# A routed transformer block: expert blocks of 256 rows instead of 128, and gate and placement moved behind the second turn of the attention output

## The reference

```
h = embed(x)                                  # [64, 197, 192]: 196 patches and a class token
h = h + attention(layernorm(h))               # 12 heads of 16, q and k normalised a head
x2 = layernorm(h).reshape(12608, 192)
scores = sigmoid(x2 @ gate_weight.T)          # 8 experts in 4 groups
# 2 groups by the sum of their biased scores, then the 2 best experts in them
w, idx = chosen scores over their sum, their experts
h1, h3 = x2 @ w1[e].T, x2 @ w3[e].T           # 128 wide
y = sum over the 2 chosen e of  w * (silu(h1) * h3) @ w2[e].T
z = silu(x2 @ sw1.T) * (x2 @ sw3.T) @ sw2.T   # the shared expert, every row
h = h + y + z
```

## Time and profile before

| | us |
|---|---|
| median of 3 runs (lowest, highest) | 2247.59 (2235.23, 2253.08) |
| the profiled execution, its span | 2258.84, 2257.0 |
| PE busy | 1861.1 (82%) |
| DVE, ACT, POOL busy | 1147.4, 992.2, 644.1 |
| phase A, to the first operation of the table | 1574.65 |
| the table | 18.07 |
| phase B's blocks | 664.28 |

### The profile page before, as it was taken

One profiled execution on the slowest core, in us unless ns is written; L12 is line 12 of the kernel. 1 busy time (PEld: TensorE's weight loads), 2 busy tenths in 40 slices (PEclk: granted clock), 3 DMA queues, 4 the chain that ended last, 5 costly groups with the idle time before them and its releaser, 6 DMA issues. The chain is left out here.

```text
span 2257.0 us, 56485 instructions
## 1 busy us (share of the span) xinstructions
PE 1861.1 (82%) x16989; PEld 1447.9 (64%) x16990; DVE 1147.4 (51%) x4105; ACT 992.2 (44%) x2620; POOL 644.1 (29%) x681
## 2 busy tenths in 40 slices
PE   3988889898988988989898898973677888788886
PEld 2767777776776766777677677753455555555554
DVE  3465666665765665666566566654422222222222
ACT  2544445554554544455455454540233333333333
POOL 2011121211212121121122112122244444444444
PEclk9998999999999999999899999995555555555555
DMA  4011111111111111111111111101343444443443
GB/s 140 23 39 39 53 45 44 54 53 40 51 47 46 53 43 42 53 45 53 41 46 56 42 53 45 32 27 34 58 63 61 63 62 61 62 63 59 60 63 43
DMA packets 97206, 116.35 MB, mean 52 GB/s; under 512 B 16496, under 2 KB 83700, under 8 KB 96884
## 3 DMA queue, kind: packets, MB, share of 16 engines
q1 hardware_dynamic: 55108, 74.15, 11.7%
q0 software_dynamic: 41872, 39.30, 11.0%
HBM read 63.65 MB, written 50.51 MB: 51 GB/s over the span
## 5 line engine op out<-in xcount | busy, mean ns | idle before, releaser
L1457 POOL DMA_INDIRECT out<-yb,xb x205 | 319.5, 1558 | 363.8 <-ACT yb L1357 187.8
L772 ACT ACTIVATE prob<-ps_sc 99x792 f32<-99x792 f32 x384 | 317.2, 826 | 220.0 <-PE ps_sc L532 217.1
L474 PE MATMUL ps_hid<-lin_f,xin 128*99 128x192 f32 x1536 | 305.1, 345 | 79.6 <-DVE v L927 44.8
L474 PEld LDWEIGHTS ps_hid<-lin_f,xin 128*99 128x99 f32 x1536 | 249.9, 175 | 92.6 <-issue 56.3
L1434 DVE TENSOR_TENSOR in_lo<-inner,in_hi 128x128 f16<-128x128 f32 x205 | 59.9, 292 | 478.4 <-ACT in_hi L1350 477.1
L1300 PE MATMUL ps_h<-bT_hi,w_hi 96*128 96x128 f16 x820 | 251.3, 306 | 57.1 <-issue 47.9
L1153 POOL DMA_INDIRECT dispatch<-rows,slot x256 | 254.0, 992 | 123.1 <-issue 63.1
L1301 PE MATMUL ps_h<-bT_lo,w_hi 96*128 96x128 f16 x820 | 257.2, 314 | 0.0
L1302 PE MATMUL ps_h<-bT_hi,w_lo 96*128 96x128 f16 x820 | 257.2, 314 | 0.0
L1147 POOL CAST slot<-slot_f 99x4 int32<-99x4 f32 x64 | 11.6, 181 | 821.4 <-DVE slot_f L1049 821.4
L532 PE MATMUL ps_sc<-qT,kT 32*99 32x198 f32 x3072 | 192.6, 368 | 14.5 <-issue 11.8
(11 more groups left out here) (172 smaller groups left out, 4113.6 us busy)
## 6 DMA issues: line engine op xcount, KB each, us to landing
xin<-xp SPq DMA_DIRECT2D x64, 594.0 KB, 3.9
xb<-dispatch SPq DMA_DIRECT2D x205, 98.0 KB
out<-base SPq DMA_DIRECT2D x64, 147.0 KB
dispatch<-rows,slot POOLq DMA_INDIRECT x256
out<-yb,xb POOLq DMA_INDIRECT x205
w_f<-w SPq DMA_DIRECT2D x1, 1728.0 KB, 12.1
out<-base SPq DMA_DIRECT2D x64, 0.8 KB
w_f<-w SPq DMA_DIRECT2D x1, 864.0 KB, 13.8
```

The lines of the kernel that those rows point to most:

```text
L474: last = pe.matmul(hid[:, t, :], xin[q][:, k, t * TR:(t + 1) * TR], lin_f[:, k, :], start=(k == 0), stop=(k == PCHUNKS - 1))
L772: act.activation(prob[quad][:, places].rearrange("p h m s -> p h (m s)"), ps_sc[0:TR, places, 0:2 * SLOTS], ACT.Exp, scale=D ** -0.5 / (SQ ...
L1457: pool.indirect_dma_start(tokens_out, bass.IndirectOffsetOnAxis(ap=xb[n.mod(XB)][:, ID_AT:ID_AT + 1].bitcast(I32), axis=0), yb[n.mod(4)][: ...
```

## The change

It has two independent parts.

**Blocks.** PARTS = 2 and BLOCK = 256. `xb`, `pad` and `yb` hold two rows a partition, PE turns a block with 4 transposes, its 12 inner products have 256 columns, its outer products are 6 matmuls, ACT weighs in two operations and POOL issues two indirect transfers a block; BLOCKS becomes 106, TABLE 109. XB becomes 4. The expert's number is read into a register once a block and kept (`expert_at`), ahead of the body's matmuls. Waits on `added` count 32 a block instead of 16.

**Phase A's order.** On PE, `shared_inner(n6)` comes before `qk(n2, 1)`; the third quad of scores comes a step earlier, behind `transpose_qk(n2, 0, 0)`; then `o_by_token(n4, 1)`, `places(n7)`, `gate(n6)` and `embed(k, 0)`. On ACT, `shared_sigmoid` comes before `square(n2, 1)` and `gate_exp` last. On DVE, all of `route` is for n7, its third part and `place_out` stand behind `v_copy`, and `shared_gate` and `residual` come before `qk_normalise(n2, 1)`.

```diff
-BLOCK = 128
+PARTS = 2
+BLOCK = 128 * PARTS
...
-XB = 8
+XB = 4
...
             def load(n):
                 if n.c >= XB or not n.known:
-                    sp.wait_ge(added[n.mod(2)], parity(n.back(XB), 32))
+                    sp.wait_ge(added[n.mod(2)], parity(n.back(XB), 16 + ADDS))
                 at = sp.value_load(entry(1, n), min_val=0, max_val=E * CAP)
-                sp.dma_start(xb[n.mod(XB)][:], dispatch[bass.DynSlice(at, BLOCK), :]).then_inc(x_in[n.mod(XB)], 16)
+                rows = dispatch[bass.DynSlice(at, BLOCK), :].rearrange("(p r) w -> p r w", r=PARTS)
+                sp.dma_start(xb[n.mod(XB)][:], rows).then_inc(x_in[n.mod(XB)], 16)
...
             def body(n):
+                inner_e = expert_at(n.back(1)) if n.back(1).active() else None
+                outer_e = expert_at(n.back(3)) if n.back(3).active() else None
                 if n.active():
                     turn(n)
                 if n.back(1).active():
-                    inner_products(n.back(1))
+                    inner_products(n.back(1), inner_e)
                 if n.back(3).active():
-                    outer_products(n.back(3))
+                    outer_products(n.back(3), outer_e)
...
-                act.activation(yb[q][:], outer[n.mod(2)], ACT.Copy,
-                               scale=xb[n.mod(XB)][:, W_AT:W_AT + 1]).then_inc(yb_done, 1)
+                for r in range(PARTS):
+                    last = act.activation(yb[q][:, r, :], outer[n.mod(2)][:, r, :], ACT.Copy,
+                                          scale=xb[n.mod(XB)][:, r, W_AT:W_AT + 1])
+                last.then_inc(yb_done, 1)
...
-                pool.indirect_dma_start(
-                    tokens_out, bass.IndirectOffsetOnAxis(ap=xb[n.mod(XB)][:, ID_AT:ID_AT + 1].bitcast(I32), axis=0),
-                    yb[n.mod(4)][:], None, bounds_check=TOTAL - 1, oob_is_err=False,
-                    compute_op=ALU.add).then_inc(added[n.mod(2)], 16)
+                for r in range(PARTS):
+                    ids = xb[n.mod(XB)][:, r, ID_AT:ID_AT + 1].bitcast(I32)
+                    pool.indirect_dma_start(
+                        tokens_out, bass.IndirectOffsetOnAxis(ap=ids, axis=0), yb[n.mod(4)][:, r, :], None,
+                        bounds_check=TOTAL - 1, oob_is_err=False,
+                        compute_op=ALU.add).then_inc(added[n.mod(2)], 16)
```

More of the change, by code:

```diff
@@ L605, in gate, with places @@
                 last.then_inc(gate_done, 1)
-            def places(n, attended, turned):
+            def places(n, attended, before, turned):
                 pe.wait_ge(taken_done, n.times(1, 1))
[L610 to L613, removed]
+                o_bank_read(attended, before, turned)
                 here = slice(0, TR - 1)
@@ L622, in shared_inner @@
             def shared_inner(n, embedded):
+                pe.wait_ge(yT_set, n.times(1, 1))
                 if embedded.active():
@@ L644, in step @@
             def step(k):
-                n1, n2, n3, n4, n5, n6, n7 = (k.back(d) for d in (1, 2, 3, 4, 5, 6, 7))
+                n1, n2, n3, n4, n5, n6, n7, n8 = (k.back(d) for d in range(1, 9))
                 if n4.active():
-                    scores(n4, 2)
-                    attend(n4, 1, None, None, None)
+                    attend(n4, 1, None, n7, n8)
                 if n3.active():
@@ L683, in step @@
                     attend(n4, 2, n6, None, None)
+                if n6.active():
+                    shared_inner(n6, n1)
                 if n2.active():
@@ L687, in step @@
                     project(n5)
[L689 to L694, removed]
                 if n3.active():
                     scores(n3, 1)
-                    attend(n3, 0, None, n6, n7)
+                    attend(n3, 0, None, None, None)
                 if n4.active():
@@ L705, in step @@
                     transpose_qk(n2, 0, 0)
+                if n3.active():
+                    scores(n3, 2)
+                if n4.active():
+                    o_by_token(n4, 1, n5, n2)
+                if n7.active():
+                    places(n7, n3, n4, n6)
+                if n6.active():
+                    gate(n6, n3, n4)
                 if k.active():
                     embed(k, 0)
-                if n4.active():
-                    o_by_token(n4, 1, n5, n2)
             run(pe.Fori, step)
@@ L859, in step @@
                     qT_copy(n2, 0)
+                if n6.active():
+                    gate_exp(n6)
             run(act.Fori, step)
@@ L1069, in step @@
             def step(k):
-                n1, n2, n3, n4, n5, n6, n7 = (k.back(d) for d in (1, 2, 3, 4, 5, 6, 7))
+                n1, n2, n3, n4, n5, n6, n7, n8 = (k.back(d) for d in range(1, 9))
                 if n5.active():
                     o_out(n5, 1)
+                if n3.active():
+                    kT_copy(n3, 0)
                 if n6.active():
                     rows_out(n6)
-                if n3.active():
-                    kT_copy(n3, 0)
                 if n2.active():
@@ L1200, in phase_b @@
         table = sb("table", [1, 3, TABLE], I32)
-        xb = [sb(f"xb{p}", [BLOCK, ROW]) for p in range(XB)]
+        xb = [sb(f"xb{p}", [128, PARTS, ROW]) for p in range(XB)]
         bT_hi = [sb(f"bT_hi{p}", [KC, 2, BLOCK], F16) for p in range(2)]
@@ L1208, in phase_b @@
         in_lo = [sb(f"in_lo{p}", [INTER, BLOCK], F16) for p in range(2)]
-        yb = [sb(f"yb{p}", [BLOCK, C]) for p in range(4)]
+        yb = [sb(f"yb{p}", [128, PARTS, C]) for p in range(4)]
         ps_t = [ps(f"ps_t{p}", [128, 512]) for p in range(2)]
@@ L1226, in phase_b @@
         DEPTH = 4
+        ADDS = 16 * PARTS
         def run(fori, body):
```

94 lines of the change are left out of this document (53 added, 41 removed).

## The result

The changed kernel takes 3087.2 us (median of 4 runs, 3079.3 to 3095.7) against 2243.0 us (4 runs, 2235.2 to 2253.1) for the kernel before: a ratio of 1.376, 95% interval 1.369 to 1.384. The forecast was 3040 us in a range of 2900 to 3200. The profiled execution took 3095.7 us with a span of 3092.7.

What follows compares the result with a forecast made beforehand. PE was taken to bound both phases before; with four buffers the way round the ring would bound phase B. Span 1592.7 - 100 (phase A) - 6 (table) + 1560 (phase B) = 3046 us, predicted time 3040, range 2900 to 3200.

Steps and rivals of the forecast that it cites:

- Ring, and its period: Phase B: with four buffers each block waits the whole way round; period 14.9 us, 102 blocks wait, phase B 1560 us.
- W: Phase B: PE's work on a block, first transposes to start of last outer product, 4.2 us.
- (W + L) / (XB - 3): Phase B: least period, PE's work W 4.2 us plus way round to next transposes L 10.7 us; buffers held three bodies.
- The reads of the expert's number: Phase B: reads now stand ahead of the transposes, where PE waits anyway; costed at nothing.
- Table: Block table between the phases: 109 entries instead of 208; saves 6 us.
- Phase A: Phase A's new order: gain 70 us from 1.1 us a step, plus 30 from the clock; together 100 us, between 40 and 204.
- The three waits: Phase A, PE's waits for onT_lo (0.59 us), the residual (1.00) and v_copy (0.57): removed, 2.16 us a step.
- a clean step near 20.4 us: Phase A, sign of the forecast: a clean step falls from 21.64 us to near 20.4 us.
- the part from the clock: Phase A: PE's granted clock of 0.95 rises as waits no longer stand within 3 us of each other; 30 us.
- The sum: Whole kernel: 1592.7 - 100 - 6 + 1560 = 3046 us of span; predicted time 3040 us.
- The loads stay hidden: Rival, phase B: PE sets the period, 4.9 us a block; phase B 540 us, total 2018 us; 5%.
- The clock rises in the bursts: Rival, phase B: PE's bursts get 2.4 GHz, W falls to 2.1 us, 214 us less, total 2826 us; 4%.

Runs made afterwards that it cites:

- ring5: Changed kernel with five xb buffers (XB = 5, loop unrolled 20 times, load's wait on the block five back); 2347.4 us in one run.
- before_ring4: Kernel before with XB = 4 in place of 8, blocks still of 128 rows; 3877.4 us in one run.
- ring8: Changed kernel with XB = 8 in place of 4, nothing else; 1981.4 us, ratio 0.887.
- early4: Changed kernel, still four buffers, but DVE copies weights and token numbers to a small tile and the next load waits only for that copy; 1877.3 us, ratio 0.848.
- load_once: Kernel before with the expert's number read once a block, ahead of PE's transposes, nothing else; 2113.8 us, ratio 0.952.
- order_only: Kernel before with the changed order of phase A alone, blocks and ring as before; 2212.1 us, ratio 0.9895.
- scatter_again: Changed kernel with XB = 8 and POOL's scatter held until ACT's square of the next step, run again on another chip; 1969.0 us, ratio 0.877.
- the second group: Runs on one chip beside the kernel before, among them early4, load_once and kT_first; ratios 0.848, 0.952 and 0.844.
- kT_first: ring8 with base_add and kT_copy moved ahead of qk_variance in DVE's list of phase A; 1870.2 us, ratio 0.844.
- kT_again: The kernel of kT_first, to the letter, run again on another chip; 1906.9 us, ratio 0.851.

## Why the prediction was right

**Ring, and its period: right, 14.8 us for 14.9.** By the block above: W 4.24 for 4.2; 0.40 for 0.40; to POOL 1.62 for 1.38 + 0.4 = 1.78; the second addition 1.85 for 1.86; to SP's load 4.47 for 4.25; the load 2.24 for 2.4. Six terms, each within 0.25 us. That their errors cancel is luck: all one way, they would have been 0.6 us a period, some 60 us. ring5 and before_ring4 show the formula (W + L) / (XB - 3) at two other points, ring8 that with 3.0 us from it another bound takes over, early4 that the hold makes it. The 102 periods and both ends give 1559 us behind the table's first operation, where the steps add to some 1572.

**The reads of the expert's number: right at nothing.** Under the wait for `xb` no open time of theirs is left to see. load_once shows that the new place takes most of their cost away even with no such wait: blocks away from the loop's turn went from 3.06 to 2.4 us, the two at the turn stayed long. The prediction's reading, "the gaps belong to the reads and not to the columns", holds at 1.2 GHz.

**Table: right.** One operation of the seven takes 1.05 us for 872 elements, against 1.88.

**Phase A: the step that failed.** Forecast 100 us, 41 in the two profiles, 24 in the timed comparison of order_only. The three waits went, as forecast, and the transposes behind the attention quad wait, though 0.37 us (19.2 in 52 times) and not 0.7. The sentence that failed is "POOL's scatter moves with `place_out` to the step's end; it has a whole step before the rows' buffer is wanted, so nothing." It asked only who waits for the scatter, not what runs beside it, and so the sign of a clean step near 20.4 us failed: it stayed at 21.6. On the chip of the result ACT is late beside the scatter's four transfers; in the order before that fell on ACT's h_lnvar, in the new one on yT and the square, which DVE's `qk_variance`, `base_add` and kT copy and PE's `scores` stand behind. That is 1.5 us a step, 63.9 in all. That the lateness follows the scatter is shown (scatter_again); by what way POOL's transfers reach ACT and DVE is not, and neither is it why one chip is free of it. On the chip of the second group, where ACT is not late, phase A's border lies at 1418.9 us in early4 and at 1538.4 in load_once: 119 us for the order alone, near the 100 forecast, and the granted clock of 170 to 1300 us is 0.98 against 0.95, so the part from the clock is there too. In the changed kernel it is not: 0.95 from 170 to 1500 us, as before. That it hangs on how near the waits stand to one another, as the prediction had it, no run shows.

The sum: phase A +59 us against the forecast, what follows -13, together the 46 us by which the span of 3092.7 passes the 3046 forecast. Two slips in the prediction's own working changed nothing: four operations of 0.19 us are 0.76 and not 0.7 with handovers, and the upper end of the period, "about 17", came into the range as 16.5.

**The rivals.** "The loads stay hidden" came true with XB at 8 and with the early release, not with XB at 4. The Trainium skill's rule ("Trainium Kernel Development and Optimization", Best Practices) to double-buffer for overlap would have been content with 4; the wait of 1083.6 us speaks against reading it as enough. "The clock rises in the bursts" did not happen at a period of 14.8 us (0.55 in phase B), but did at 7.4 (0.70 in ring5 from 1600 to 1950 us) and with ring8 (0.90).

## What to carry to other kernels

Count a ring's depth in rounds: how many bodies a buffer is held, plus the whole way round (last reader, write-back landing, the wait, the reload) over the period. When blocks double, keep the number of buffers and not their bytes, unless the period grows as much; or copy out the few columns that late readers need, and free the buffer at once. And when a reordering moves a transfer, ask not only who waits for it but which engine works beside it in its new place, and compare on more than one chip. And two equal sums of idle time need not be the same idle time: look at single blocks before you say that it only moved.

## What the hardware showed that I had not expected

- ACT starts instructions 1 to 2 us late (1.4, 1.7 and 1.9 in the rows above), with nothing ahead of them, while four indirect transfers of POOL are under way or just over, and DVE's `base_add` beside them 1.2 us late: on three of the four chips of the experiments. On the fourth, with the same program, it doesn't (kT_first: no such wait on the square; kT_again: 53.8 us). For that program it is 1906.9 against 1870.2 us. Between ring8 (1981.4) and early4 (1877.3), whose phases A are the same, lie 104 us, while the kernel before is only 19 us apart on these two chips (2236.1, 2217.2).
- PE's granted clock in phase B is 0.50 in the kernel before, where PE was busy 79% of the stretch, 0.74 in load_once at 78%, and 0.90 in ring8 at 70%. And 2.4 GHz gave load_once's blocks nothing: 2.40 us against 2.42 at 1.2 GHz.
- A read of a table entry on PE's queue left 0.23 and 0.27 us open in front of each of two runs of matmuls. Once a block and ahead of the transposes, a block at 1.2 GHz takes 2.38 us without a gap, against 3.04. The sums of "issue" time, 112.3 us before and 112.7 in load_once, are alike by chance: the second is made of long gaps at the loop's turn and of gaps in the stretches at 2.4 GHz.
